# Two graph layers over one pass through a 64 MB adjacency matrix: turns of 256 rows for 512, runs of 2 KB for 1 KB

## The chip, the cores and the metric

The kernel runs on one core of one Trainium2 chip. Its engines work side by side and wait for each other through semaphores: TensorE (PE, with its weight loads listed apart as PEld), VectorE (DVE), ScalarE (ACT), GpSimd (POOL), and SyncE (SP), which here only issues transfers; POOL issues some too. All transfers run on the core's 16 DMA engines. The metric is the time of one execution on the device, in microseconds (us). Everything is computed in float32.

## The reference

`adj` is 4096 x 4096, mostly zero, with a full diagonal; `x` is 4096 x 128. Cut to what matters:

```
h   = relu(layernorm(x))
msg = h @ W0 + B
w   = where(adj < 1, exp(-(1/adj - 1)**2 / 0.5), 0)
x   = x + w @ msg                       # layer 0
h   = relu(layernorm(x))
A   = adj + I;  d = rowsum(A) ** -0.5
x   = x + relu((d[:,None] * A * d[None,:]) @ (h @ W1.T))    # layer 1
```

Layer 1's product needs `support = d * (h @ W1.T)` of all rows of x, and so layer 0 of all rows; both layers need every element of `adj`.

## The kernel before, in words

`adj` (64 MB) is read once. Its rows come in `G` = 8 turns of 512 rows. A turn has four pairs; `load(n)` on SP (L274) brings pair n, 512 rows by 1024 columns, as four DMAs of 512 KB, each into 32 of the 128 partitions of one of the `RAW` = 2 buffers `raw`, in contiguous runs of `W` = 256 floats (1 KB). A pair is two units u, each 512 x 512, a tile of 128 x 2048 floats. `UNITS` = 64.

For each unit DVE turns it in 32 x 32 blocks (`turn`, L648: `kept` <- `raw`, `KEPT` = 4 buffers), and masks it (`cut`, L663: `wt` <- `kept`, `WTS` = 6 buffers). ACT makes the weights in place in four passes (log L528, 1/adj L533, square L538, exp L547); for every second unit of the first three turns DVE does the square (`quad`, L669). PE multiplies the weights with `msg` into the PSUM bank `acc0` (`multiply_weights`, L377, `LAG` = 3 units behind). In turns 0 to 2 PE sums the rows of adj (L407); from turn 3 (`PE_SUMS`) DVE does, straight from `raw`, both units of a pair in one reduction (`row_sum`, L656).

When all 8 units of turn g-1 are in `acc0`, a chain of small steps makes 512 rows of `support` during turn g: ACT copies acc0 out (`copy_x1t`, L573), PE turns it (`turn_x1`, L430), DVE adds x and normalizes (`make_x1`, L745), PE turns and multiplies it (L436, L442), ACT copies and takes powers, DVE scales (`make_support`, L774).

Layer 1 uses the same adj tiles. A unit whose column block's support exists (`at_once`) is multiplied from `kept` (`mix_once`, L390). All others are stored to DRAM (`store`, L291, 1 MB each, 35 of them), read back later by POOL (L345) into one of `LATE` = 3 buffers `late`, or, at the end, into the parts of `raw`, and multiplied then (`mix_late`, L399) in places written out by hand (`JOBS`, `TAIL`). The PSUM banks at the end are turned back, scaled, passed through relu, added to x and written.

What sets the order is the order in which each engine's queue is written; no scheduler moves anything. `load(n)` waits until pair n-2 is turned, and from turn 3 on until its `row_sum` is done too. `turn(u)` waits until unit u-4 is out of `kept` (stored or multiplied). PE's next `acc0` sum waits for `copy_x1t`, and `turn_x1` waits in addition for `own_rows` (DVE, L736), which reads the row sums from the same bank.

## Time and profile before

| | |
|---|---|
| median of 3 runs | 662.49 us (662.48 to 664.77) |
| the profiled execution | 667.09 us, span 665.3 us |
| PE busy | 542.6 us, 82% |
| DVE busy | 485.1 us, 73% |
| ACT busy | 466.5 us, 70% |
| POOL busy | 39.6 us, 6% |
| mean granted TensorE clock | 0.921 of 2.4 GHz |
| DMA | 145.14 MB, mean 218 GB/s |

The span goes from the first to the last instruction of the profiled execution, and its own time is 1.8 us longer. It is 4.6 us above the median of the other runs. Busy time is the sum over the span, and says nothing about where an engine waits; a stage with its own limit has to be read by itself. Matmul ends are modelled, so starts are used below, not durations. An f32 matmul is two instructions in the trace and one in the program's order.

### The profile page before, as it was taken

The page shows a single profiled execution, that of the slowest core. Times are in us where ns is not written, and L with a number is a line of the kernel's source. Part 1 is how long each engine was busy: PE and PEld are TensorE (multiplying, and loading weights), DVE is VectorE, ACT ScalarE, POOL GpSimd, SP SyncE. Part 2 cuts the span into 40 slices and gives each one's busy share as a digit, 9 for nine tenths or more (in the row PEclk, how much of TensorE's full clock was granted, in tenths as well). Part 3 has the DMA queues.
Part 4 walks back from the last instruction along what each step waited for, and adds up shares of the span by engine and source line. Part 5 has one row for each costly group of instructions (what it writes and reads, how often), then busy time and mean ns, then how long its engine had stood idle before and what let it go on. Part 6 is the DMA issues. An engine that isn't in the chain of part 4 may idle for free.

```text
span 665.3 us, 4420 instructions
## 1 busy us (share of the span) xinstructions
PE 542.6 (82%) x1509; PEld 246.7 (37%) x1509; DVE 485.1 (73%) x555; ACT 466.5 (70%) x306; POOL 39.6 (6%) x68
## 2 busy tenths in 40 slices
PE   0548777699778975698496999699989999899995
PEld 0324423233233432243243434344435444344442
DVE  2899967796678997789596996699378956501156
ACT  0568968888859698969966996699596993750010
POOL 0432200000000000000000000000000000011100
PEclk9968797799778997989697999799999999999999
DMA  8999999999999599969998699969976971186713
GB/s 159 199 268 270 325 273 280 283 271 284 251 285 236 102 287 274 271 111 260 270 228 190 125 199 295 258 152 222 301 196 147 222 158 64 63 339 225 257 50 78
DMA packets 87193, 145.14 MB, mean 218 GB/s; under 512 B 4225, under 2 KB 78210, under 8 KB 78210
## 3 DMA queue, kind: packets, MB, share of 16 engines
q1 hardware_dynamic: 82130, 108.15, 71.3%
q0 software_dynamic: 5040, 36.70, 15.7%
q8 instruction: 12, 0.20, 0.1%
q14 instruction: 11, 0.09, 0.0%
HBM read 106.04 MB, written 38.80 MB: 218 GB/s over the span
## 4 chain that ended last, share of the span: by engine, by line
PE 30%; ACT 28%; DVE 17%; DMA 12%; issue 6%; SPq 6%; DVEq 0%
DMA raw<-in_adj_dram 12%; PE mix L399 10%; PE acc L377 9%; ACT wt L528 7%; ACT wt L547 7%; ACT wt L538 7%; ACT wt L533 7%; PE mix L390 6%; DVE kept L648 5%; SPq L281 5%; DVE wt L663 4%; DVE wt L669 2%; PE side L442 2%; PE acc L399 2%; PE side L399 1%
## 5 line engine op out<-in xcount | busy, mean ns | idle before, releaser
L377 PE MATMUL acc<-wt,msg 128*128 128x512 f32 x512 | 251.1, 637 | 35.2 <-ACT x1t L573 35.2
L528 ACT ACTIVATE wt<-wt 128x2048 f32<-128x2048 f32 x64 | 122.0, 1906 | 107.4 <-DVE wt L663 107.4
L648 DVE STREAM_TRANSPOSE kept<-raw 128x2048 f32<-128x2048 f32 x64 | 147.6, 2306 | 40.5 <-DMA raw<-in_adj_dram 27.5
L377 PEld LDWEIGHTS acc<-wt,msg 128*128 128x128 f32 x512 | 102.2, 206 | 172.7 <-issue 128.6
L663 DVE SCALAR_TENSOR_TENSOR wt<-kept 128x2048 f32<-128x2048 f32 x64 | 146.5, 2289 | 1.5
L533 ACT ACTIVATE wt<-wt 128x2048 f32<-128x2048 f32 x64 | 121.5, 1898 | 0.3
L390 PE MATMUL mix<-kept,support 128*128 128x512 f32 x224 | 101.5, 598 | 2.0 <-ACT mixed L589 1.7
L547 ACT ACTIVATE wt<-wt 128x2048 f32<-128x2048 f32 x52 | 98.5, 1895 | 0.0
L538 ACT ACTIVATE wt<-wt 128x2048 f32<-128x2048 f32 x52 | 98.5, 1894 | 0.0
L399 PE MATMUL mix<-late,support 128*128 128x512 f32 x200 | 90.8, 598 | 0.0
L656 DVE TENSOR_REDUCE rowpart<-raw 128x16 f32<-128x4096 f32 x20 | 87.6, 4378 | 0.0
L390 PEld LDWEIGHTS mix<-kept,support 128*128 128x128 f32 x224 | 42.2, 192 | 55.0 <-issue 53.0
L399 PEld LDWEIGHTS mix<-late,support 128*128 128x128 f32 x200 | 38.5, 193 | 48.0 <-issue 48.0
L745 DVE TENSOR_TENSOR x<-side,x 128x512 f32<-128x512 f32 x8 | 5.5, 691 | 65.1 <-PE side L430 65.1
L345 POOL DMA_DIRECT2D late<-adj_t_spill x27 | 14.4, 535 | 525.4 <-PE mix L399 425.4
L407 PE MATMUL mix<-kept,ones 128*32 128x512 f32 x192 | 30.8, 722 | 10.0 <-DVE kept L648 10.0
L442 PE MATMUL side<-w1t,hid_t 128*128 128x128 f32 x64 | 12.7, 361 | 25.8 <-ACT hid_t L585 25.8
L669 DVE SCALAR_TENSOR_TENSOR wt<-wt 128x2048 f32<-128x2048 f32 x12 | 27.4, 2282 | 0.0
L632 ACT COPY kept<-mix 128x512 f32<-128x512 f32 x6 | 3.5, 585 | 29.9 <-PE mix L399 26.6
L330 POOL TENSOR_SCALAR support<-x,mv 128x128 f32<-128x128 f32 x24 | 20.1, 856 | 48.2 <-DVE mv L688 48.2
L442 PEld LDWEIGHTS side<-w1t,hid_t 128*128 128x128 f32 x64 | 11.2, 259 | 31.7 <-ACT hid_t L585 30.8
L544 ACT ACTIVATE wt<-wt 128x2048 f32<-128x2048 f32 x12 | 22.7, 1895 | 0.0
(87 smaller groups left out, 247.0 us busy)
## 6 DMA issues: line engine op xcount, KB each, us to landing
raw<-in_adj_dram SPq DMA_DIRECT2D x128, 512.0 KB, 12.4
adj_t_spill<-kept SPq DMA_DIRECT2D x35, 1024.0 KB, 14.0
late<-adj_t_spill POOLq DMA_DIRECT2D x27, 1024.0 KB, 10.1
raw<-adj_t_spill POOLq DMA_DIRECT2D x8, 1024.0 KB, 6.1
x<-in_x_dram SPq DMA_DIRECT2D x32, 64.0 KB, 7.6
out_dram<-kept SPq DMA_DIRECT2D x32, 64.0 KB, 1.8
w_sb<-in_L_gnn_W_dram SPq DMA_DIRECT2D x1, 64.0 KB
late<-in_L_gnn_W_dram SPq DMA_DIRECT2D x1, 64.0 KB
```

The source lines that it names most:

```text
L377: mm = nc.tensor.matmul(acc0[:], msg[:, col(u) * T + k, :], wt[:, u % WTS, k, :], start=(first and k == 0), stop=(last and k == T - 1))
L390: mm = nc.tensor.matmul(once_bank[g][:], support[:, c * T + k, :], kept[:, u % KEPT, k, :], start=(first and k == 0), stop=False)
L399: mm = nc.tensor.matmul(bank[:], support[:, c * T + k, :], late_tile(slot)[:, k, :], start=(start and k == 0), stop=(stop and k == T - 1))
L442: mm = nc.tensor.matmul(side[:, a * P:(a + 1) * P], hid_t[:, a * P:(a + 1) * P], w1t[:], start=True, stop=True)
L528: nc.scalar.activation(v, v, ACT.Ln, bias=LN_GUARD).then_inc(ln_done, 1)
L533: nc.scalar.activation(v, v, ACT.Exp, scale=-1.0).then_inc(inv_done, 1)
L538: nc.scalar.activation(v, v, ACT.Square, bias=-1.0).then_inc(square_done, 1)
L547: nc.scalar.activation(v, v, ACT.Exp, scale=-2.0).then_inc(wt_done, 1)
L648: nc.vector.transpose(dst, src).then_inc(turned, 1)
L656: nc.vector.tensor_reduce(dst, src, AX_X, ALU.add).then_inc(summed, 1)
L663: nc.vector.scalar_tensor_tensor(out=wt[:, u % WTS], in0=v, scalar=CUTOFF, in1=v, op0=ALU.is_lt, op1=ALU.mult).then_inc(cut_done, 1)
L669: nc.vector.scalar_tensor_tensor(out=v, in0=v, scalar=-2.0, in1=v, op0=ALU.add, op1=ALU.mult).then_inc(quad_done, 1)
```

## The change

Rows now come in `G` = 16 turns of 256 rows. A turn has two loads l (`C2` = 2), each 256 rows by 2048 columns: still 2 MB in four DMAs into 32 partitions each, now in runs of 512 floats (2 KB). A load has two units, which are still 128 x 2048: `cut`, the passes on ACT and their buffers keep their size and number. `kept` has 2 buffers of a whole load; a load is turned in two halves (one for each k), each of which holds a part of all its eight 256 x 256 blocks. All 64 `turn` are shifted: the second half of load l stands at the head of unit 2l, the first half of load l+1 at the head of unit 2l+1. `row_sum` goes by halves, 40 of 2048 elements per partition in place of 20 of 4096, one behind each `cut` from turn 6 on.

A block of adj is multiplied at once only if its support is two turns old (c <= g-2). The others are stored in one DMA per load, up to 2 MB, and read back in pieces of one or two blocks (256 or 512 KB) into 6 smaller `late` buffers. `acc0` has two halves, one for each parity of the turn, so the next turn's sum no longer waits for this turn's copy. The chain's steps are respaced: copy, `own_rows`, `turn_x1` and `make_x1` in turn g+1, `multiply_support` and `make_support` in turn g+2. Every matmul of `acc0` and `mix` has 256 columns in place of 512, and there are twice as many. `LAG` is 2. At the start SP issues the weights' DMAs ahead of x and adj. The final relu moves from DVE to ACT.

```diff
-G = 8
-C4 = 4
+G = 16
+C2 = 2
-T = 4
-RAW, KEPT, WTS, LATE = 2, 4, 6, 3
-LAG = 3
+T = 2
+H = 8
+PART = 4
+RAW, KEPT, WTS, LATE = 2, 2, 6, 6
+LAG = 2
...
-PE_SUMS = 3
+PE_SUMS = 6
...
-            def load(n):
-                g = n // C4
-                if n >= RAW:
-                    if n - RAW >= PE_SUMS * C4:
-                        sp.wait_ge(summed, n - RAW + 1 - PE_SUMS * C4)
-                    sp.wait_ge(turned, 2 * (n - RAW + 1))
+            def load(l):
+                g = l // C2
+                if l >= RAW:
+                    sp.wait_ge(turned, 2 * (l - RAW) + 2)
+                    if l - RAW >= PE_SUMS * C2:
+                        sp.wait_ge(summed, 2 * (l - RAW + 1 - PE_SUMS * C2))
                 for q in range(Q):
-                    sp.dma_start(raw[q * B:(q + 1) * B, n % RAW],
-                                 adj_parts[g // 2, g % 2, col(2 * n) // 2, q]).then_inc(raw_loaded[n % RAW], 16)
+                    sp.dma_start(raw[q * B:(q + 1) * B, l % RAW],
+                                 adj_parts[g // H, g % H, c_of(l), q]).then_inc(raw_loaded[l % RAW], 16)
...
+                if u % 4 == 0 and g >= 2:
+                    pe.wait_ge(x1t_copied, g - 1)
+                for a in range(PART * T):
+                    mm = nc.tensor.matmul(acc0[:, g % 2, :], msg[:, blocks(u)[0] * T + a, :], wt[:, u % WTS, a, :],
+                                          start=(u % 4 == 0 and a == 0), stop=(u % 4 == 3 and a == PART * T - 1))
...
+                g, idx = u // 4, u % 4
+                l = u // 2
+                if u % 2 == 0:
+                    turn(l, 1)
+                elif l + 1 < LOADS:
+                    turn(l + 1, 0)
+                cut(u)
+                if u >= 1 and squared_by_dve(u - 1):
                     quad(u - 1)
-                if idx % 2 == 1 and g >= PE_SUMS:
-                    row_sum(u // 2)
+                if g >= PE_SUMS:
+                    row_sum(l, u % 2)
...
+                if g >= 2 and idx == 1:
+                    make_support(g - 2)
                 if g >= 1 and idx == 3:
                     own_rows(g - 1)
-                if g >= 1 and idx == 5:
                     make_x1(g - 1)
-                if g >= 1 and idx == 7:
-                    make_support(g - 1)
-                if g >= PE_SUMS:
-                    cut(u)
```

Two places carry most of it. First DVE in the second half of the program, from one `row_sum` to the first turn of the same `raw` buffer's next contents. Before (L648 turn, L663 cut, L656 row_sum of a whole pair, L736 and L739 own_rows; `raw_loaded` is the wait for adj):

```order
L656 TENSOR_REDUCE rowpart<-raw 128x4x4 [waits quads_summed]
L663 SCALAR_TENSOR_TENSOR wt<-kept 128x2048 [waits acc0_done,turned]
L648 STREAM_TRANSPOSE kept<-raw 128x16x4x32 [waits once_done,raw_loaded1]
L663 SCALAR_TENSOR_TENSOR wt<-kept 128x2048 [waits acc0_done,turned]
L648 STREAM_TRANSPOSE kept<-raw 128x16x4x32 [waits once_done]
L656 TENSOR_REDUCE rowpart<-raw 128x4x4
L736 TENSOR_TENSOR rowown<-side,own_quad 128x64 [waits newton,quads_summed]
L739 TENSOR_REDUCE pows<-rowown 128x4 [waits rows_owned]
L663 SCALAR_TENSOR_TENSOR wt<-kept 128x2048 [waits acc0_done,turned]
L648 STREAM_TRANSPOSE kept<-raw 128x16x4x32 [waits once_done,raw_loaded0]
```

Of the change (L728 turn, L747 cut, L736 row_sum of half a load, L757 to L857 make_support):

```order
L728 STREAM_TRANSPOSE kept<-raw 128x8x8x32 [waits once_done,spilled1,raw_loaded1]
L747 SCALAR_TENSOR_TENSOR wt<-kept 128x2048 [waits acc0_done,turned]
L736 TENSOR_REDUCE rowpart<-raw 128x2x2
L757 TENSOR_TENSOR tmp<-inv 128x4 [waits pows_exp]
L759 SCALAR_TENSOR_TENSOR tmp<-tmp,pows 128x4 [waits newton]
L762 SCALAR_TENSOR_TENSOR inv<-tmp,inv 128x4 [waits newton]
...
L728 STREAM_TRANSPOSE kept<-raw 128x8x8x32
L747 SCALAR_TENSOR_TENSOR wt<-kept 128x2048 [waits acc0_done,turned]
L736 TENSOR_REDUCE rowpart<-raw 128x2x2
L728 STREAM_TRANSPOSE kept<-raw 128x8x8x32 [waits spilled0,raw_loaded0]
```

Before, buffer 0 is done at the first row, and turned again at the last: three cuts, two turns and another whole reduction stand between them. In the change the last read of buffer 0 is the third row, one turn ahead of which stands the first turn of buffer 1; from there to buffer 0's next turn stand one turn, one cut, half a reduction and a chain step.

Second SP at the same stage: what each load waits for. Before:

```order
L291 DMA adj_t_spill<-kept 128x2048 [waits turned] x2
L281 DMA raw<-in_adj_dram 32x16x256 [waits turned,summed]
L281 DMA raw<-in_adj_dram 32x16x256 x3
L291 DMA adj_t_spill<-kept 128x2048 [waits turned]
L281 DMA raw<-in_adj_dram 32x16x256 [waits turned,summed]
L281 DMA raw<-in_adj_dram 32x16x256 x3
```

Of the change:

```order
L323 DMA adj_t_spill<-kept 128x1024 [waits turned]
L309 DMA raw<-in_adj_dram 32x8x512 [waits summed,turned]
L309 DMA raw<-in_adj_dram 32x8x512 x3
L323 DMA adj_t_spill<-kept 128x4096 [waits turned]
L309 DMA raw<-in_adj_dram 32x8x512 [waits summed,turned]
L309 DMA raw<-in_adj_dram 32x8x512 x3
```

The waits have the same names and each load has four DMAs of 32 partitions in both; what moved is the place on DVE at which `summed` is reached.

Third PE at the last support but one (L413 weights, L426 mix at once, L438 mix late, L478 turn_x1, L484 turn_hid). Before, the corresponding chain (L430) stands in the middle of the last turn:

```order
L430 MATMUL side<-ident,x1t 128x128 [waits rows_owned,x1t_copied]
L430 MATMUL side<-ident,x1t 128x128 x3
L377 MATMUL acc<-wt,msg 128x512 [waits wt_done]
L377 MATMUL acc<-wt,msg 128x512 x3
L390 MATMUL mix<-kept,support 128x512 [waits turned]
L390 MATMUL mix<-kept,support 128x512 x3
```

Of the change:

```order
L478 MATMUL side<-ident,x1t 128x128 [waits rows_owned,x1t_copied]
L478 MATMUL side<-ident,x1t 128x128
L438 MATMUL mix<-late,support 128x256 [waits sup_done,late_loaded4]
L438 MATMUL mix<-late,support 128x256 x3
L438 MATMUL mix<-late,support 128x256 [waits sup_done,late_loaded5]
L438 MATMUL mix<-late,support 128x256 x3
L426 MATMUL mix<-kept,support 128x256 [waits sup_done,turned]
L426 MATMUL mix<-kept,support 128x256 x3
L413 MATMUL acc<-wt,msg 128x256 [waits wt_done]
L413 MATMUL acc<-wt,msg 128x256 x7
L484 MATMUL side<-ident,hid 128x128 [waits hid_done]
```

The first row waits for `own_rows`, which DVE in the change reaches only after the last unit's cut and row sum; the weights of the last three units and the whole tail are behind it on PE.

## Rows read from the trace of the kernel before

**Rows 1.** The chain of waits by engine and line, whole span (page, part 4).

```profile
PE 30%; ACT 28%; DVE 17%; DMA 12%; issue 6%; SPq 6%; DVEq 0%
```

**Rows 2.** Busy time by stage: us, busy of PE, PEld, DVE, ACT, POOL, PEclk, DMA share, GB/s.

```profile
88.00:220.00 132.00, 107.20 (x334) 41.60 (x333) 101.95 (x91) 105.86 (x67) 1.05 (x2) 0.87 1.06 270
220.00:573.00 353.00, 304.99 (x745) 139.29 (x743) 286.62 (x220) 286.74 (x177) 9.51 (x18) 0.94 0.86 205
336.80:407.20 70.40, 63.11 (x155) 28.91 (x154) 58.14 (x48) 58.97 (x36) 1.58 (x3) 0.95 0.88 196
```

**Rows 3.** Waits: who waited for whom, us in total, times, longest.

```profile
ACT wt L528 <- DVE wt L663: 107.4, 31, 11.4
DVE x L745 <- PE side L430: 65.1, 7, 24.0
PE acc L377 <- ACT x1t L573: 35.2, 5, 11.4
```

**Rows 4.** DVE's timeline from a row sum to the same buffer's next turn.

```profile
366.49 4.38 DVE L656 TENSOR_REDUCE rowpart<-raw 128x16 f32<-128x4096 f32 x1
370.78 2.28 DVE L663 SCALAR_TENSOR_TENSOR wt<-kept 128x2048 f32<-128x2048 f32 x1
372.98 2.30 DVE L648 STREAM_TRANSPOSE kept<-raw 128x2048 f32<-128x2048 f32 x1
375.32 2.29 DVE L663 SCALAR_TENSOR_TENSOR wt<-kept 128x2048 f32<-128x2048 f32 x1
...
386.63 2.31 DVE L648 STREAM_TRANSPOSE kept<-raw 128x2048 f32<-128x2048 f32 x1
```

**Rows 5.** L281's issues and landings for one load, window 370 to 372.6.

```profile
L281 SPq DMA_DIRECT2D raw<-in_adj_dram x4: 312/488/490, 370.9 to 372.3; - x4
DMA to landing us min/median/max: 5.0/8.4/12.5
```

**Rows 6.** The same for two other loads, windows 299 to 302 and 512 to 520.

```profile
L281 SPq DMA_DIRECT2D raw<-in_adj_dram x4: 312/488/499, 299.1 to 300.5; - x4
DMA to landing us min/median/max: 5.0/8.4/11.5
...
L281 SPq DMA_DIRECT2D raw<-in_adj_dram x4: 311/486/489, 515.3 to 516.7; - x4
DMA to landing us min/median/max: 5.0/8.4/14.2
```

**Rows 7.** Transfers of 373 to 381 us: adj alone, runs of 1 KB.

```profile
DMA packets 1627, 1.62 MB, mean 202 GB/s; under 512 B 48, under 2 KB 1627, under 8 KB 1627
```

**Rows 8.** Transfers of 31 to 35 us: x alone, runs of 512 B, also 32 partitions.

```profile
DMA packets 1812, 0.84 MB, mean 209 GB/s; under 512 B 201, under 2 KB 1811, under 8 KB 1811
```

**Rows 9.** Transfers of 586 to 594 us: reads of the spill, 8 KB, 128 partitions.

```profile
DMA packets 467, 3.43 MB, mean 429 GB/s; under 512 B 48, under 2 KB 48, under 8 KB 48
```

**Rows 10.** DVE's timeline, where turn 2 ends and row sums begin.

```profile
218.13 2.31 DVE L648 STREAM_TRANSPOSE kept<-raw 128x2048 f32<-128x2048 f32 x1 [1.44 <-DMA raw<-in_adj_dram]
220.36 2.25 DVE L669 SCALAR_TENSOR_TENSOR wt<-wt 128x2048 f32<-128x2048 f32 x1
222.53 2.28 DVE L663 SCALAR_TENSOR_TENSOR wt<-kept 128x2048 f32<-128x2048 f32 x1
...
226.96 4.38 DVE L656 TENSOR_REDUCE rowpart<-raw 128x16 f32<-128x4096 f32 x1
```

**Rows 11.** DVE's timeline, the last cut.

```profile
577.50 2.28 DVE L663 SCALAR_TENSOR_TENSOR wt<-kept 128x2048 f32<-128x2048 f32 x1
```

**Rows 12.** The chain's end, in order of time.

```profile
649.20 3.44 PE acc L399 x8
652.63 0.44 PE mix L488 x4
653.07 3.45 PE side L399 x8
656.52 0.02 issue
661.01 0.69 DVE kept L824
```

**Rows 13.** PE's timeline in the tail: 128-column matmuls and what follows.

```profile
618.48 1.05 PE L442 MATMUL side<-w1t,hid_t 128*128 128x128 f32 x8
619.37 1.45 PE L399 MATMUL acc<-raw,support 128*128 128x512 f32 x3
```

**Rows 14.** ACT's timeline: two passes in a row.

```profile
363.45 1.90 ACT L533 ACTIVATE wt<-wt 128x2048 f32<-128x2048 f32 x1
365.25 1.89 ACT L547 ACTIVATE wt<-wt 128x2048 f32<-128x2048 f32 x1
```

More of the change, by code:

```diff
@@ L99, in late_slot @@
         return j % LATE
-    tail = [(len(IN_TURN) + i) % LATE for i in range(LATE)] + [LATE + i for i in range(2 * RAW)]
+    tail = [(len(IN_TURN) + i) % LATE for i in range(LATE)] + [LATE + i for i in range(4 * RAW)]
     return tail[(j - len(IN_TURN)) % len(tail)]
@@ L367, in multiply_msg @@
                 last.then_inc(m_multiplied, 1)
             def multiply_weights(u):
-                first, last = u % G == 0, u % G == G - 1
+                g = u // 4
                 pe.wait_ge(wt_done, u + 1)
-                if u < G and u % 2 == 0:
-                    pe.wait_ge(msg_done, u // 2 + 1)
-                if first and u >= G:
-                    pe.wait_ge(x1t_copied, u // G)
-                for k in range(T):
-                    mm = nc.tensor.matmul(acc0[:], msg[:, col(u) * T + k, :], wt[:, u % WTS, k, :],
-                                          start=(first and k == 0), stop=(last and k == T - 1))
+                if g == 0:
+                    pe.wait_ge(msg_done, blocks(u)[0] // PART + 1)
@@ L384, in mix_once @@
[L384 to L391 removed]
+                r = u // 4
@@ new lines, in mix_once @@
+                pe.wait_ge(turned, 2 * (u // 2) + 2)
+                pe.wait_ge(sup_done, at_once(u)[-1] + 1)
+                first = r % 2 == 0 and once_count(u // 2 - 1) + (u % 2 and bool(at_once(u - 1))) == once_count(2 * r - 1)
+                if first and r >= 12:
+                    pe.wait_ge(evicted, r // 2 - 5)
+                for c in at_once(u):
+                    for k in range(T):
+                        mm = nc.tensor.matmul(turn_bank[r // 2][:, r % 2, :], support[:, c * T + k, :],
+                                              kept[:, u // 2 % KEPT, c % H, k, :],
+                                              start=(first and c == at_once(u)[0] and k == 0), stop=False)
@@ L401, in mix_late @@
                 mm.then_inc(late_done, 1)
             def sum_tiles(u):
-                pe.wait_ge(turned, u + 1)
-                bank = sum_bank[u // G]
-                for k in range(T):
-                    mm = nc.tensor.matmul(bank[k * B:(k + 1) * B, :], ones[:], kept[:, u % KEPT, k, :],
-                                          start=(u % G == 0), stop=(u % G == G - 1))
+                pe.wait_ge(turned, 2 * (u // 2) + 2)
+                g = u // 4
+                if u % 4 == 0 and g >= 2:
+                    pe.wait_ge(sums_copied, g - 1)
@@ L462, in _ @@
                 if g < PE_SUMS:
                     sum_tiles(u)
-                if at_once(u) and idx < G - 1 and not (g >= 6 and idx == 0):
+                if at_once(u):
                     mix_once(u)
-                if g >= 1 and idx == 4:
-                    turn_x1(g - 1)
+                if g >= 1 and idx == 2:
+                    if g <= PE_SUMS:
+                        add_sums(g - 1)
+                    else:
+                        add_quads(g - 1)
                 if u >= LAG:
@@ new lines, in copy_h0 @@
+            def copy_h0(s):
+                act.wait_ge(h0_turned, s + 1)
+                if s >= 1:
+                    act.wait_ge(m_multiplied, s)
+                nc.scalar.copy(h0_t[0], h0_bank[0][:].rearrange("p r j -> p (r j)"))
+                nc.scalar.copy(h0_t[1], h0_bank[1][:].rearrange("p r j -> p (r j)")).then_inc(h0_t_done, 1)
+            def copy_sums(g):
+                act.wait_ge(tiles_summed, 4 * (g + 1))
+                if g >= 1:
+                    act.wait_ge(rows_added, g)
+                for k in range(T):
+                    last = nc.scalar.copy(in_tiles(sums[:, k]), by_tile(sum_bank[g % 2][:, k, :]))
+                last.then_inc(sums_copied, 1)
@@ new lines, in relu_out @@
+            def relu_out(i):
+                b = ENDS[i]
+                act.wait_ge(out_summed, i + 1)
+                for a in range(2 * T):
+                    v = fin[i % 4][:, a * D:(a + 1) * D]
+                    n = b * 2 * T + a
+                    last = nc.scalar.activation(v, v, ACT.Relu, scale=dinv[:, n:n + 1])
+                last.then_inc(out_relu, 1)
+            for i, b in enumerate(ENDS):
+                if b >= 2:
+                    take_mix(i)
+                if i >= 2:
+                    relu_out(i - 2)
```

646 lines of the change are left out of this document (341 added, 305 removed), and 4 rows, old and new, of the table JOBS.

## The prediction, made before the result was known

> **What bounds the kernel now.** I read the chain of waits first: no engine holds a third of it [rows 1], so the stages have to be read apart. From 88 to 220 us the DMA share is 1.06 (over 1, since transfers of two queues overlap) while DVE and ACT are busy 102 and 106 of 132 us [rows 2]: transfers bind. From 220 to 573 us it is 0.86, and PE, DVE and ACT have 305, 287 and 287 of 353 us; one turn lasts 70.4 us with PE 63.1, ACT 59.0 and DVE 58.1 in it. What is missing there is in the table of waits [rows 3]: DVE stands in `make_x1` for PE's `turn_x1` (65.1 us in 7 waits), so the next cut is late and ACT idles (107.4 us, up to 11.4 a time); PE waits 35.2 us for acc0's copy. After 573 us PE works off a backlog.
>
> The wait that does not show is the one for adj. On DVE's timeline [rows 4] a row sum starts at 366.49, the next instruction at 370.78, and the turn that needs the same buffer again at 386.63: 15.8 us. The load issued at 370.9 landed at 372.3 + 12.5 = 384.8, 13.9 us after its first issue [rows 5]; two others took 300.5 + 11.5 - 299.1 = 12.9 us and 516.7 + 14.2 - 515.3 = 15.6 us [rows 6]. The mean is 14.1 us. So the load is hidden, with under 2 us to spare.
>
> **The change: the load's cover.** From turn 6 on, load l+2 is issued when DVE has finished the second half sum of load l. In DVE's new order that half sum stands behind the first turn of load l+1, which waits for load l+1 to land. So load l+2 cannot be issued before load l+1 has landed: the two buffers no longer overlap, and one load is in flight at a time. The period of a load is its latency, plus a turn, a cut and a half sum. By starts in [rows 4] a turn takes 2.34 us, a cut 2.21, a whole sum 4.29, so a half 2.15: together 6.7 us. What else DVE has in a period (another 6.7 us, and a chain step of 1.4 or about 3 us) lies inside the latency.
>
> **The latency with 2 KB runs.** The trace has no 2 KB runs. Adj's 1 KB runs alone moved at 202 GB/s [rows 7]; x's runs of 512 B at 209 GB/s [rows 8]. Halving the run cost nothing, so I see no cost per run that doubling it could save. Both go into 32 partitions per DMA, as the change's loads still do. The spill's reads, 8 KB runs into 128 partitions, made 429 GB/s [rows 9]; they differ in two things, and the pair above speaks for the partitions. A load of 2.10 MB at 202 GB/s is 10.4 us, at 209 it is 10.0: I take 0.4 us off, 14.1 - 0.4 = 13.7 us, and a period of 20.4 us. Bounds: below, 8 KB's rate, 2.10 / 0.429 = 4.9 us in place of 10.4, latency 8.6 us, period 15.3 (DVE's own work is then 2 x 6.7 + 2.3 = 15.7, and binds); above, no gain from runs, 20.8. By the spread of [rows 5, 6], which comes from other transfers in flight, the period is 12.5 + 6.7 = 19.2 to 15.6 + 6.7 = 22.3.
>
> The Trainium skill ("SBUF — State Buffer", section "Door 1: The DMA port swizzle") says that a DMA into partitions 0 to 31 reaches 8 of the 16 ports, 189 GB/s measured at 1 MiB and about 218 at best, whatever its runs. The trace agrees with 202 and 209. By its 218 GB/s a load's transfer would be an estimated 9.6 us and the period 19.9, 9 us less in the sum.
>
> **How often it is paid.** Loads 14 to 31 wait for half sums. From the issue of load 14 to that of load 31 are 17 periods, 347 us; load 31 lands 13.7 us later; then DVE has turn, cut, half sum (6.7), `make_support` (1.4), the same three (6.7) and the last cut (2.2): 17.0 us.
>
> **When it begins.** Before, unit 24 is turned at 218.1 us, waiting for adj, and the first row sum starts at 226.96 [rows 10]. Up to there the change moves as many bytes: the same 24 units of adj, and 86 spilled blocks of 0.25 MB (21.5 MB) for 21 stores of 1 MB. The weights' three DMAs now ahead of adj cost 1.4 us, and turn 0 has the same work on x in half as many units, some 2 us that the transfers don't cover. With 8 x 0.4 us back from the runs I put that landing at 218. Then stand turn and cut (4.5), a chain step (3), turn, cut, quad and half sum (6.7 + 2.2), and a turn, cut and half sum (6.7), and slack of 1 for the load between: 240 us. The last cut ends at 240 + 347 + 13.7 + 17.0 = 618 us; before it ends at 577.5 + 2.3 = 579.8 [rows 11].
>
> **The tail.** In the change `turn_x1` of turn 14 waits for `own_rows`, which follows the last cut by a half sum and 0.6 us: PE stands until 2.8 us after the cut. Behind it are 10 blocks and three units' weights, and then TAIL with 57 blocks. Eight 512-column instructions take 3.44 us [rows 12], 430 ns each. A unit's weights are 3.44 us as before; a block is 4 of 256 columns, 0.86. 67 x 0.86 + 3 x 3.44 = 68 us, with 5 for the small matmuls and the output's 32 transposes, 2.8 before, and 3 for half clock after the stand: 79. From the last product's end to the end it is now 665.3 - 656.5 = 8.8 us [rows 12]; with eight output DMAs for four, 9. So 88 us, against 665.3 - 579.8 = 85.5.
>
> Sum: 618 + 88 = 706 us of span; before 665.3.
>
> **What I cost at nothing.** Matmuls of 256 columns: in the tail eight of 128 columns start at 618.48, and what follows at 619.37 [rows 13], 111 ns each where 430 / 4 is 107. So a weight load per 128 columns is hidden, and 4 ns is the price of an instruction. 1024 more of them are 4 us of PE, which waits anyway; 0.5 in the tail are counted. ACT: passes start 1.80 us apart [rows 14], 14.4 us a load with 1 for small copies: under 20.4. DVE's extra small steps, 2 us a turn: inside the latency. If the cover went, ACT and DVE would bind at about 15.7 us a load. The doubled acc0 and the chain's wider spacing do remove the waits of [rows 3], up to 11.4 us in each of five turns, but nobody gets that time: DVE now stands for adj instead. PE has 13.8 us of weights in a turn, up to 26 blocks (22.4) and 1: 37 us in the last turns, against two periods of 40.8.
>
> **Rivals.** First, *2 KB runs are much faster*, which ends below before. If the 1 KB run's 81 ns (1024 B at a sixteenth of 202 GB/s) and the 8 KB run's 305 ns (429) lie on one line, 2 KB is 113 ns, 290 GB/s, 7.2 us: period 17.2, in the early stage 15 us less (ACT then holds it), so 225 + 292 + 10.5 + 17 + 88 = 633. At 429 GB/s: 218 + 267 + 9 + 17 + 88 = 599, plus some 10 for PE's last turns. It decides from a period below 18.6 us, a load's transfer under 8.6 us or 244 GB/s. For it speaks that runs and partitions change together in [rows 7, 9]; against it [rows 7, 8]. Chance 0.19.
>
> Second, *PE becomes the bound* in the last turns: after each stand for `own_rows` it runs at half clock for a while (PEclk is 0.94 on the mean of the middle stage [rows 2] with shorter stands). Five more us in 37 pass 40.8: up to 20 us in four turns, 715 to 735. Chance 0.10.
>
> Third, *adj's rows are read at a wider step*: one DMA now steps 4 MB from run to run, before 1 MB. Adj with 1 MB steps and x with 512 B steps move alike [rows 7, 8], so I see no cost. If it halved the rate, a period would be 20.4 + 10 = 30, and the sum 240 + 35 + 510 + 24 + 17 + 88 = 914. Chance 0.03. The Trainium skill ("DMA: Bandwidth & Descriptors", section "Latency and other measured facts") lists 164 GB/s at a row pitch of 2 MiB and 103 at 4 MiB for copies within DRAM; no run here shows it yet.
>
> Fourth, *a middle case*: the transfer falls to 8.5 to 9 us and nothing is left to tell: 655 to 670. Chance 0.05.
>
> **The numbers.** The profiled execution's own time is 667.1, 1.8 above its span, and 4.6 above the median of 662.5. So 706 + 1.8 - 4.6 = 703. The forecast as worked out has chance 0.63; its own range takes the period's 19.2 to 22.3: 18 x -1.2 = -22 and 18 x 1.9 = +34, 681 to 737. For 8 in 10 the range goes down to the first rival's upper case, 640, and up to 737. Faster than before by over 0.5% (about what a measurement of this kernel can tell from no change) 0.21, within it 0.04, slower 0.75.
>
> **What would show it.** Right: from about 240 us L309's groups of four are issued 20 us apart, each right behind a second half sum, never two in flight; the last of each lands some 12 us after its issue; DVE's wait for raw, 27.5 us before, is then 18 times about 4.7, some 85 us; the waits of [rows 3] at `acc` and `x` are gone or small, ACT's wait for the cut is larger; the last cut ends near 618. Wrong: adj alone moving at 250 GB/s or more, issues 16 to 18 us apart, or PE busy through the second half. The step I trust least is the rate of 2 KB runs; each microsecond there is 18 in the sum.

## The result, and the profile after

| | before | after |
|---|---|---|
| median | 663.57 us (4 runs, 662.48 to 664.77) | 766.53 us (4 runs, 763.73 to 772.95) |
| profiled execution, span | 667.09, 665.3 us | 766.08, 764.3 us |
| PE, DVE, ACT busy | 542.6, 485.1, 466.5 us | 567.4, 489.3, 484.1 us |
| mean granted TensorE clock | 0.921 | 0.876 |

The ratio is 1.157, 95% interval 1.149 to 1.164: slower, as forecast, but 64 us beyond the forecast's 703 and outside its range of 640 to 737. Medians in the experiments leave out executions in a slower state, such as one of `e16` with 939.3 us at a granted clock of 0.56, the only one of that kernel with a trace. Rows of after, beside [rows 1] and [rows 3]. The page's chain of waits, by engine and by line:

```profile
DMA 50%; DVE 21%; PE 9%; issue 8%; SPq 8%; POOL 2%; ACT 1%; DVEq 0%; ACTq 0%
DMA raw<-in_adj_dram 49%; DVE wt L747 8%; DVE rowpart L736 6%; SPq L309 5%; PE mix L438 4%; DVE kept L728 3%; SPq L346 2%; POOL support L364 2%; PE acc L413 1%; PE acc L438 1%; PE mix L400 1%; DVE msg L795 1%; PE mix L391 0%; PE side L478 0%; SPq L317 0%
```

The waits (us in total, times, longest):

```profile
DVE kept L728 <- DMA raw<-in_adj_dram: 165.7, 28, 9.6
ACT wt L581 <- DVE wt L747: 157.3, 43, 13.2
PE side L478 <- DVE rowown L819: 72.8, 9, 13.2
```

Before, no engine held a third of the chain; now transfers hold half and one line's load nearly all of it. What the change was built to remove is gone: PE's wait for acc0 has no row, and DVE's for PE in `make_x1` is 14.6 us where it was 65.1. DVE stands for adj instead, ACT for DVE, and PE for `own_rows`.

One period in order of time, the chain of waits from 401 to 423 us (start, us, what):

```profile
401.26 2.25 DVE wt L747
403.51 2.21 DVE rowpart L736
...
405.78 0.31 SPq L309
...
407.12 15.73 DMA raw<-in_adj_dram
...
422.91 2.20 issue
```

A cut, the second half sum, and only then the next load's four issues; DVE's next turn starts at 422.88, 17.1 us after the first issue. SP's timeline gives the periods. The first of these groups is load 14, the last load 31:

```profile
248.58 2.74 SPq L309 DMA_DIRECT2D raw<-in_adj_dram  x4
...
635.37 2.66 SPq L309 DMA_DIRECT2D raw<-in_adj_dram  x4
```

(635.37 - 248.58) / 17 = 22.75 us a load, where 20.4 was forecast. DVE's timeline from load 31's landing to the last cut:

```profile
652.66 2.31 DVE L728 STREAM_TRANSPOSE kept<-raw 128x2048 f32<-128x2048 f32 x1 [8.16 <-DMA raw<-in_adj_dram]
...
667.38 2.28 DVE L747 SCALAR_TENSOR_TENSOR wt<-kept 128x2048 f32<-128x2048 f32 x1
```

and the end, PE's timeline (the last product), SP's (the output) and DVE's (the last steps):

```profile
738.03 7.07 PE L438 MATMUL side<-raw,support 128*128 128x256 f32 x32
```
```profile
731.70 30.96 SPq L346 DMA_DIRECT2D out_dram<-kept  x64
```
```profile
748.88 0.69 DVE L909 TENSOR_TENSOR kept<-side,support 128x512 f32<-128x512 f32 x1 [1.78 <-DMA out_dram<-kept]
...
750.91 0.69 DVE L916 TENSOR_TENSOR kept<-kept,x 128x512 f32<-128x512 f32 x1 [0.74 <-ACT kept L702]
```

DVE is done at 751.6, but SP still issues 32 KB writes until 762.7, 484 ns apart. The span against my sum, term by term:

| term | forecast | measured | off by |
|---|---|---|---|
| issue of load 14 | 240 | 248.6 | +8.6 |
| 17 periods | 347 | 386.8 | +39.8 |
| load 31, issue to turn | 13.7 | 17.3 | +3.6 |
| from there to the last cut's end | 17.0 | 17.0 | 0 |
| last cut to the last product | 79 | 75.3 | -3.7 |
| last product to the end | 9 | 19.4 | +10.4 |
| span | 706 | 764.3 | +58.3 |

So the mechanism stands (one load in flight, a period of latency plus 6.7 us) and two sizes are wrong: the latency, and the end. The experiments ask whether the mechanism is really the cost, what lengthens the latency, and what holds the end. The kernel before was run beside each group; medians of it were 662.2 to 664.0 us, and ratios are to it.

### The profile page after: what moved, and what is told of

Same layout as the page of the kernel before. It is cut to its first block, busy times and chain, and to the rows that moved or that the text cites. A ratio compares the mean times of both kernels' runs of the same rounds, so it can differ in the third digit from the quotient of the medians.

```text
span 764.3 us, 6963 instructions
## 1 busy us (share of the span) xinstructions
PE 567.4 (74%) x2567; PEld 462.4 (60%) x2567; DVE 489.3 (64%) x604; ACT 484.1 (63%) x387; POOL 67.7 (9%) x124
## 3 DMA queue, kind: packets, MB, share of 16 engines
q0 software_dynamic: 10992, 39.07, 16.8%
## 4 chain that ended last, share of the span: by engine, by line
DMA 50%; DVE 21%; PE 9%; issue 8%; SPq 8%; POOL 2%; ACT 1%; DVEq 0%; ACTq 0%
DMA raw<-in_adj_dram 49%; DVE wt L747 8%; DVE rowpart L736 6%; SPq L309 5%; PE mix L438 4%; DVE kept L728 3%; SPq L346 2%; POOL support L364 2%; PE acc L413 1%; PE acc L438 1%; PE mix L400 1%; DVE msg L795 1%; PE mix L391 0%; PE side L478 0%; SPq L317 0%
## 5 line engine op out<-in xcount | busy, mean ns | idle before, releaser
L728 DVE STREAM_TRANSPOSE kept<-raw 128x2048 f32<-128x2048 f32 x64 | 147.5, 2306 | 165.7 <-DMA raw<-in_adj_dram 165.7
L413 PE MATMUL acc<-wt,msg 128*128 128x256 f32 x1024 | 243.8, 393 | 8.6 <-ACT wt L600 6.5
L413 PEld LDWEIGHTS acc<-wt,msg 128*128 128x128 f32 x1024 | 199.1, 197 | 49.3 <-issue 9.4
L747 DVE SCALAR_TENSOR_TENSOR wt<-kept 128x2048 f32<-128x2048 f32 x64 | 145.4, 2272 | 1.1
L438 PE MATMUL mix<-late,support 128*128 128x256 f32 x464 | 124.2, 422 | 0.0
L426 PE MATMUL mix<-kept,support 128*128 128x256 f32 x420 | 105.1, 405 | 20.3 <-DVE kept L728 14.6
L426 PEld LDWEIGHTS mix<-kept,support 128*128 128x128 f32 x420 | 85.6, 206 | 39.3 <-DVE kept L728 15.8
L438 PEld LDWEIGHTS mix<-late,support 128*128 128x128 f32 x464 | 97.4, 217 | 14.3
L736 DVE TENSOR_REDUCE rowpart<-raw 128x4 f32<-128x2048 f32 x40 | 91.1, 2278 | 0.0
L380 POOL DMA_DIRECT2D late<-adj_t_spill x68 | 36.2, 533 | 609.0 <-PE mix L438 512.0
L478 PE MATMUL side<-ident,x1t 128*128 128x128 f32 x32 | 9.3, 387 | 101.6 <-DVE rowown L819 72.8
L478 PEld LDWEIGHTS side<-ident,x1t 128*128 128x128 f32 x32 | 4.3, 184 | 107.3 <-issue 107.2
L391 PE MATMUL mix<-ident,support 128*128 128x128 f32 x32 | 6.7, 381 | 22.6 <-POOL support L364 15.6
L597 ACT ACTIVATE wt<-wt 128x2048 f32<-128x2048 f32 x12 | 22.8, 1902 | 0.0
```

Of the source, the lines that this page charges most:

```text
L380: pool.dma_start(late_tile(slot)[:, 0:n].rearrange("p c k j -> p (c k j)"), spill[r, c // H][:, h * BLK:(h + n) * BLK]).then_inc(late_load ...
L413: mm = nc.tensor.matmul(acc0[:, g % 2, :], msg[:, blocks(u)[0] * T + a, :], wt[:, u % WTS, a, :], start=(u % 4 == 0 and a == 0), stop=(u % ...
L426: mm = nc.tensor.matmul(turn_bank[r // 2][:, r % 2, :], support[:, c * T + k, :], kept[:, u // 2 % KEPT, c % H, k, :], start=(first and c ...
L438: mm = nc.tensor.matmul(bank[:, r % 2, :], support[:, (c + b) * T + k, :], late_tile(slot)[:, b, k, :], start=(start and b == 0 and k == 0 ...
L728: nc.vector.transpose(dst, src).then_inc(turned, 1)
L736: nc.vector.tensor_reduce(dst, src, AX_X, ALU.add).then_inc(summed, 1)
```

## Experiments

**Is it the cover? One row moved on DVE.** `e1_sum_first`:

```diff
+                if g >= PE_SUMS and u % 2 == 1:
+                    row_sum(l, 1)
                 if u % 2 == 0:
                     turn(l, 1)
                 elif l + 1 < LOADS:
                     turn(l + 1, 0)
                 cut(u)
...
-                if g >= PE_SUMS:
-                    row_sum(l, u % 2)
+                if g >= PE_SUMS and u % 2 == 0:
+                    row_sum(l, 0)
```

> The changed kernel with one row moved on DVE: the second half sum of load l stands ahead of the first turn of load l+1, so load l+2 can be issued while load l+1 is still in flight. Theory A (the lost cover costs the time; the engines would allow less): the period of a load falls from 22.75 us to 16 to 17 us, set by DVE's own 15.7 us and ACT's 15; over 17 periods that is 100 us less, 655 to 680 us. Rival B (a load's transfer is slow by itself, so two in flight only share the engines): the period stays above 20 us and the time at 720 to 766 us.

Measured: 692.6 us, ratio 1.044 (1.036 to 1.051). Its waits:

```profile
DVE kept L728 <- DMA raw<-in_adj_dram: 61.5, 19, 8.9
ACT wt L581 <- DVE wt L747: 66.4, 26, 12.5
```

and loads 14 and 31 on SP:

```profile
240.24 2.79 SPq L309 DMA_DIRECT2D raw<-in_adj_dram  x4
...
552.52 2.72 SPq L309 DMA_DIRECT2D raw<-in_adj_dram  x4
```

The period is 312.3 / 17 = 18.4 us and 74 of the 103 lost us are back. The place of that one row is most of the loss. But the period isn't the 16 to 17 us of theory A: it lies between A and rival B. What holds it there this run doesn't say. A slow load is a small part of it: with nearer rows on top (`e8` below) the period is (538.41 - 236.45) / 17 = 17.8 us, and only with another order on PE (`e15`) is it (519.88 - 230.81) / 17 = 17.0.

**The same loss made in the kernel before.** `e2_before_held`:

```diff
-                    sp.wait_ge(turned, 2 * (n - RAW + 1))
+                    sp.wait_ge(turned, 2 * n if n - RAW >= PE_SUMS * C4 else 2 * (n - RAW + 1))
```

> The kernel before, with nothing but a later issue of its loads: from turn 3 on, load n waits until both units of pair n-1 are turned, so that one load is in flight at a time and 6.8 us of DVE's work (turn, cut, turn) stand between a landing and the next issue, about as in the change. Runs stay 1 KB and the rest of the kernel is untouched. If the cover alone costs the time: period 14.1 + 6.8 = 20.9 us, 240 + 17 x 20.9 + 14 + 13.5 + 85.5 = 708 us of span, about 705 us. If a load that is alone takes 16 us in this form too (so 2 KB runs aren't to blame): period 22.8, about 740 us. If the cover doesn't matter: 663 us.

Measured: 713.3 us, ratio 1.076 (1.068 to 1.084). SP's timeline from load 14's row on; 14 loads lie ahead of the last row shown, whose group is itself four loads:

```profile
232.09 2.51 SPq L281 DMA_DIRECT2D raw<-in_adj_dram  x4
...
525.08 66.13 SPq L281 DMA_DIRECT2D raw<-in_adj_dram  x16
```

(525.08 - 232.09) / 14 = 20.9 us: the period expected of this run, with the 14.1 us of latency that [rows 5, 6] give; the time is 8 us above the 705 expected. So the rule "latency plus DVE's work" and its 14.1 us hold where the runs are 1 KB and their rows 1 MB apart. In the change the latency is about 16.

**Is it the run's length?** `e3_1k_runs`, the change with each load in two halves of its columns:

```diff
-                for q in range(Q):
-                    sp.dma_start(raw[q * B:(q + 1) * B, l % RAW],
-                                 adj_parts[g // H, g % H, c_of(l), q]).then_inc(raw_loaded[l % RAW], 16)
+                for s in range(2):
+                    v = slice(s * W // 2, (s + 1) * W // 2)
+                    for q in range(Q):
+                        sp.dma_start(raw[q * B:(q + 1) * B, l % RAW, :, v],
+                                     adj_parts[g // H, g % H, c_of(l), q][:, :, v]).then_inc(raw_loaded[l % RAW], 16)
...
-                    dve.wait_ge(raw_loaded[l % RAW], 64 * (l // RAW + 1))
+                    dve.wait_ge(raw_loaded[l % RAW], 128 * (l // RAW + 1))
```

> The changed kernel with each of its loads cut into eight DMAs of 1 KB runs for four of 2 KB, with the same bytes, places and waits. Theory A (the latency of 16 us comes from what else is in flight and from the tail of the slowest engine, not from the run's length): the period stays at 22 to 24 us and the time at 755 to 790 us, more rather than less since SP issues four more DMAs of 0.4 us. Rival C (2 KB runs, or what goes with them, are slower than 1 KB): the period falls by some 2.3 us and the time to about 725 us.

Measured: 778.4 us, ratio 1.172 (1.162 to 1.183). No gain: not the length. **The loads by themselves**, `e4_loads_alone`, one 2 MB load at a time (L50 2 KB runs 8 MB apart, L55 1 KB and 1 MB, L61 1 KB and 8 MB, L66 2 KB and 2 MB, L71 and L78 the first two with a store). L50, L61 and L71 were meant to be the change's form, and the expectation calls them 4 MB. They aren't: their pattern is

```python
adj_w = adj.rearrange("(e g i) (C q w) -> g C q i e w", e=8, g=16, i=B, C=2, q=4)
```

in which one step of `e` is 16 x 32 = 512 rows of 16 KB, 8 MB. In the change it is 8 x 32 = 256 rows, 4 MB. So no run measures a 4 MB step by itself, and where the expectations from here on say 4 MB of a load alone, 8 MB was run.

> Measures the disputed cost by itself; it computes nothing and writes zeros. Loads of 2 MB into 32 partitions per DMA, one at a time, nothing else in flight: 2 KB runs 4 MB apart (the change's), 1 KB runs 1 MB apart (the one before), 1 KB runs 4 MB apart (eight DMAs), 2 KB runs 2 MB apart; then the first two forms again with a 2 MB store from 128 partitions issued right behind each load. If run length is to blame for the late landing: 14 us and more for 2 KB against 12 for 1 KB. If the step is: 4 MB slower than 1 MB at either length. If only what else is in flight is: all four near 12 us alone, and 15 to 18 us with the store.

SP's timeline; six loads a row, four for L66:

```profile
18.94 73.37 SPq L50 DMA_DIRECT2D wide<-in_adj_dram  x24
103.33 61.62 SPq L55 DMA_DIRECT2D narrow<-in_adj_dram  x24
175.06 72.46 SPq L61 DMA_DIRECT2D wide<-in_adj_dram  x48
255.88 37.61 SPq L66 DMA_DIRECT2D wide<-in_adj_dram  x16
303.31 2.63 SPq L71 DMA_DIRECT2D wide<-in_adj_dram  x4
...
418.41 1.90 SPq L78 DMA_DIRECT2D narrow<-in_adj_dram  x4
...
518.95 0.41 SPq L83 DMA_DIRECT2D out_dram<-zeros  x1
```

From one row's start to the next's, divided by its loads: 14.07 us for 2 KB and 8 MB, 11.96 for 1 KB and 1 MB, 13.47 for 1 KB and 8 MB, 11.86 for 2 KB and 2 MB. 2 KB runs are no faster than 1 KB; 8 MB between a partition's eight rows costs 1.5 to 2.2 us a load. With a 2 MB store beside it the 8 MB form takes (418.41 - 303.31) / 6 = 19.2 us and the one before (518.95 - 418.41) / 6 = 16.8: traffic adds 5 to both, and the difference stays. That the change's 4 MB cost as much is the guess that the next run tests in the kernel.

**The step in the kernel.** `e5_near_rows`, order as in the change:

```diff
-        adj_parts = adj.rearrange("(R e h i) (C q w) -> R h C q i e w", e=8, h=H, i=B, C=C2, q=Q)
+        adj_parts = adj.rearrange("(R h e i) (C q w) -> R h C q i e w", e=8, h=H, i=B, C=C2, q=Q)
```

> The changed kernel, reading other rows: the 256 rows of a turn stand next to each other in adj, so that one DMA steps 512 KB from run to run and not 4 MB; all else, the order on DVE too, is the change's. It computes with the rows of adj in another order, so its output is another one. By itself a load with a 4 MB step took 14.1 us from issue to issue and one with 2 MB 11.9 (the run of loads alone). Theory A (the step is the mis-sized part of the latency): the period falls from 22.75 by some 2.2 us, over 17 periods and load 31 about 40 us, and 5 more in the stage that transfers bind: 715 to 730 us. Rival B (the late landing comes from stores and spill reads in flight or from uneven engines): 755 to 770 us.

Measured: 725.5 us, ratio 1.094 (1.087 to 1.100). Loads 14 and 31:

```profile
239.51 1.80 SPq L309 DMA_DIRECT2D raw<-in_adj_dram  x4
...
593.11 1.79 SPq L309 DMA_DIRECT2D raw<-in_adj_dram  x4
```

Load 14 is issued at 239.5, 9.1 us earlier than in the change (I had said 240), and the period is 353.6 / 17 = 20.80 us (I had said 20.4). The step alone is 9.1 + 17 x 1.95 = 42 of the 58 us that I missed; the medians differ by 41.0 us. Of the 9.1 us some may be chance: DVE first turns load 12 at 225.7 us in the change and at 216.7 here, but at 221.8 in `e1`, whose program is the change's up to there.

**Other forms of a load**, `e6_forms_alone` and `e7_first_by_row`. The second is `e1` with:

```diff
-        adj_parts = adj.rearrange("(R e h i) (C q w) -> R h C q i e w", e=8, h=H, i=B, C=C2, q=Q)
+        adj_parts = adj.rearrange("(R e h i) (C q w) -> R h C e q i w", e=8, h=H, i=B, C=C2, q=Q)
...
-                for q in range(Q):
-                    sp.dma_start(raw[q * B:(q + 1) * B, l % RAW],
-                                 adj_parts[g // H, g % H, c_of(l), q]).then_inc(raw_loaded[l % RAW], 16)
+                for e in range(8):
+                    sp.dma_start(raw[:, l % RAW, e],
+                                 adj_parts[g // H, g % H, c_of(l), e]).then_inc(raw_loaded[l % RAW], 16)
```

and with DVE's wait counting to 128 for 64, as in `e3`.

> Loads of 2 MB in 2 KB runs by themselves again, six of each form, computing nothing: the change's (rows 4 MB apart, four DMAs of 32 partitions); 256 neighbouring rows (512 KB apart, same four DMAs); rows in pairs of 512 KB within 8 MB, eight DMAs of 32 partitions; the change's rows with one DMA per run of all 128 partitions (eight DMAs, neighbouring descriptors 2 or 16 KB apart); and two of the change's and two of the near loads in flight at once. If the step costs: the first takes 14.1 us, the second 11.9 or less. If the 32 partitions of a DMA hold the rate at about 200 GB/s: the form by all 128 partitions takes 7 to 9 us in place of 14; if the step or the whole of the engines holds it, 11 us or more. Two near loads at once, if the 200 GB/s are one load's own limit: under 20 us for both; if a shared one: 21 us and more.

> The change with the second half sum ahead of the next load's turn, as in the run that gave 692.6 us, and with each load as eight DMAs, one per row of all 128 partitions, for four of 32 partitions and eight rows. The same output as the change. If the form removes the cost of the 4 MB step or of the 32 partitions: DVE's wait for adj, 61.5 us there, falls to 20 or less: 655 to 675 us. If eight issues on SP (some 3.5 us a load) or the same rate as before eat it: 690 to 705 us.

`e6` on SP: six repeats in each of L53 (`adj_w` as in `e4`, 8 MB apart and not the change's 4), L58 (512 KB apart), L65 (pairs), L70 (one DMA per row of L53's), L76 and L83 (two of the first, two of the second at once):

```profile
18.95 73.44 SPq L53 DMA_DIRECT2D wide<-in_adj_dram  x24
103.07 62.90 SPq L58 DMA_DIRECT2D wide<-in_adj_dram  x24
175.95 63.67 SPq L65 DMA_DIRECT2D wide<-in_adj_dram  x48
247.66 130.52 SPq L70 DMA_DIRECT2D wide<-in_adj_dram  x48
388.94 128.00 SPq L76 DMA_DIRECT2D wide<-in_adj_dram  x48
533.49 112.61 SPq L83 DMA_DIRECT2D wide<-in_adj_dram  x48
664.06 0.42 SPq L87 DMA_DIRECT2D out_dram<-zeros  x1
```

14.0, 12.1, 11.9, 23.5, and 24.1 and 21.8 for two at once (12.0 and 10.9 each). The form in pairs is as fast as near rows, although each of its eight DMAs steps 8 MB from run to run too; it has four runs per partition for eight, and the near row of each pair is in another DMA. So a wide step by itself doesn't make a load slow. Whether the number of rows at that step or the near rows in between make the difference, no run separates. Two loads at once gain little: in this form, four DMAs of 32 partitions a load, both together move at most 193 GB/s, so the overlap hides a load's latency and makes no rate. One DMA per row is by far the slowest: `e7` took 966.3 us, ratio 1.456. `e6` from 300 to 340 us, transfers:

```profile
DMA packets 1890, 3.76 MB, mean 94 GB/s; under 512 B 56, under 2 KB 56, under 8 KB 1890
```

with the 16 engines busy 0.25 of the time. The Trainium skill ("DMA: Bandwidth & Descriptors", section "Why a DMA increments its semaphore by 16 and not by 1") says that the engines a DMA uses are the largest number up to 16 that divides the slowest dimension of both its patterns. In this form adj's slowest dimension is the quarter, 4, so four of 16; the trace agrees with the share of 0.25. I had expected 7 to 9 us there from the number of partitions, and hadn't looked at the pattern's outer dimension.

**Both causes away.** `e8_first_and_near` is `e1` with the line of `e5`.

> Both causes taken away at once: the second half sum ahead of the next load's turn, and neighbouring rows (512 KB steps; adj's rows in another order, so another output). If the step and the lost cover are all that the change lost on adj, DVE's wait for it falls from 61.5 to some 20 us, and the time to 655 to 675 us, about that of the kernel before. Rival (what is left is PE or the tail): 680 to 692 us, with PE in the chain from 560 us on in either case.

Measured: 677.1 us, ratio 1.019 (1.012 to 1.025), just above the expected range, with an output in another order as in `e5`. DVE waits 35.3 us for adj in 15 waits, and the top wait of a working engine is another:

```profile
ACT x1t L626 <- PE acc L413: 59.5, 9, 14.0
```

ACT's copy of acc0 stands ahead of its passes and waits for PE's last weights of the turn, which stand behind the blocks mixed at once.

**The same with the reference's output.** `e9_paired_rows`: strips of 32 rows in neighbouring pairs (h, k, i for k, h, i in adj, x and out). A load is then eight DMAs, one for each k and q, and two runs of x and of the output merge into one DMA each. The patterns, and the load:

```diff
-        adj_parts = adj.rearrange("(R e h i) (C q w) -> R h C q i e w", e=8, h=H, i=B, C=C2, q=Q)
+        adj_parts = adj.rearrange("(R e h k i) (C q w) -> R h C q k i e w", e=Q, h=H, k=T, i=B, C=C2, q=Q)
...
-        out_parts = out.rearrange("(C q k h i) d -> C q k i h d", C=C2, q=Q, k=T, h=H, i=B)
+        out_parts = out.rearrange("(C q h k i) d -> C q i (h k) d", C=C2, q=Q, k=T, h=H, i=B)
...
+                for k in range(T):
+                    for q in range(Q):
+                        dst = raw[q * B:(q + 1) * B, l % RAW].rearrange("p (e k) w -> p k e w", k=T)[:, k]
+                        sp.dma_start(dst, adj_parts[g // H, g % H, c_of(l), q, k]).then_inc(raw_loaded[l % RAW], 16)
```

> The second half sum ahead of the next load's turn, and another order of rows and columns within a turn: 32-row strips in neighbouring pairs (rows h, k, i instead of k, h, i), in adj, x and out alike, so the output is the reference's. A load is then eight DMAs with four runs per partition, the form that took 11.95 us alone against 14.02; x needs four DMAs a part for eight, and a bank of the output four DMAs for eight (32 in all for 64). Theory: adj as fast as with neighbouring rows (677.4 us), and the end after PE's last product, 19 us with 64 output DMAs at 0.47 us each on SP, shorter by 8 to 10: 665 to 670 us. Rival (eight issues per load, some 3.5 us on SP, eat what the step gives): 675 to 690 us.

Measured: 663.1 us, ratio 1.001 (0.998 to 1.005), no different from before, and just below the expected range. The period, (533.87 - 229.50) / 17 = 17.9 us, is that of near rows. Last product to the end is 661.9 - 652.2 = 9.7 us, the 9 that I had given it, with 32 output DMAs.

**The end.** `e10_two_queues` (on `e9`) and `e12_out_by_two` (on the change) let POOL issue half of the output's DMAs; `e14_out_by_act` (on the change) lets ACT issue one half and leaves SP the other. ACT's part of `e14`:

```diff
+            def write_half(i):
+                b = ENDS[i]
+                act.wait_ge(out_done, i + 1)
+                tiles = fin[i % 4].rearrange("p (h k d) -> p k h d", h=2, k=T)
+                for q in range(Q):
+                    h = 2 * b % H
+                    act.dma_start(out_parts[2 * b // H, q, 1][:, h:h + 2],
+                                  tiles[q * B:(q + 1) * B, 1]).then_inc(out_written[i % 4], 16)
```

> The same, and half of the 32 output DMAs issued by POOL, whose queue is empty by then. If SP's issues still hold the end: 2 to 4 us less than the run before. If the last bank's own chain (turn, sum, relu, sum, write) holds it: no change.

> The changed kernel itself, with nothing but half of its 64 output DMAs issued by POOL. From PE's last product to the end it takes 19.4 us where I had forecast 9, with SP issuing from 731.7 us for 31 us. If the issues on SP are that difference: 8 to 10 us less, 756 to 759 us. If the writes themselves are slow: no change, 766 us.

> The changed kernel, half of whose 64 output DMAs are issued by ACT, each behind its bank's last step. With POOL as the second issuer the last write was issued 8 us earlier than in the change, but landed 12 us after its issue. If SP's issues are what my 9 us for the end left out and POOL's own transfers the reason that it didn't show: 756 to 759 us. If the writes are slow whoever issues them: 766 us.

Measured: 669.5 (ratio 1.013, 1.008 to 1.019), 768.0 (1.162, 1.154 to 1.169) and 755.1 us (1.143, 1.137 to 1.149). ACT's share gives 11 us: the end is SP's issues, as the 64 DMAs at 484 ns say. POOL's gives nothing in the change and costs 6 us in `e10`. In `e12` the last issue ends 8.6 us behind the last product (756.2 against 747.7), where it was 17.8 in the change: what the shorter queue gives is lost behind it. POOL's writes land 2 us after their issue, not 12 as the expectation of `e14` has it, which counted to the end of the program. The last issues and their landing are over at 758 us, but the program ends at 768.1:

```profile
753.60 2.63 POOL L387 DMA_DIRECT2D out_dram<-kept  x5
```
```profile
DMA to landing us min/median/max: 1.8/1.9/2.8
```

What runs in the last 10 us has no row; in `e10` the last POOL issue is at 655 and the end at 666.9. Why the program ends so late is open.

**What is left: PE's order.** `e11_weights_first` (on `e10`), `e13_paired_weights` (on `e9`) and `e15_weights_all` (on `e9`):

```diff
+                if u >= LAG:
+                    multiply_weights(u - LAG)
                 if at_once(u):
                     mix_once(u)
...
-                if u >= LAG:
-                    multiply_weights(u - LAG)
```

That is `e15`; in the other two it is done at the second unit of a turn only. `e16_all_three` is `e13` with half of the output issued by ACT.

> The same as the run before, and at the second unit of each turn PE does the last weights of the turn before ahead of the blocks mixed at once. In the run with near rows ACT stood 49.6 us for PE in 6 copies of acc0 between 240 and 600 us. If that stand is on the path: up to 3.45 us less in each of some 9 turns, at most 15 us and more likely 5 in all. If PE is the bound there, its order doesn't matter: no change; a loss of 2 to 5 us if the kept buffer, free 3.45 us later, holds DVE.

> Half sum first, rows in neighbouring pairs, all output DMAs on SP (663.1 us), and PE's last weights of a turn ahead of the blocks mixed at once. With POOL's half of the output this order gave 6.5 us (669.5 to 663.0). If that gain is ACT's shorter stand for acc0, it adds up: 656 to 658 us. If it was chance or POOL's end: 663 us.

> The same with the weights ahead of the blocks mixed at once in every unit, not in one of four. If ACT waits for PE's weights only at the copy of acc0: no more gain than with one of four, 656 to 660 us. If the kept buffer, free 3.45 us later each time, holds DVE's next turn: 665 to 680 us.

> Half sum first, paired rows, weights first in one unit of four, and the 32 output DMAs half on SP and half on ACT. After DVE's last step the end still takes 4.9 us with all of them on SP; four issues of 0.47 us become two: 1 to 2 us less than the run without it, 654 to 657 us, or no change if ACT's issues delay its own copies.

Measured: 663.0 us (ratio 0.999, 0.995 to 1.003), which is 6.5 below `e10`; 652.1 (0.986, 0.981 to 0.990); **641.4** (0.969, 0.965 to 0.973); 650.3 (0.984, 0.979 to 0.989). `e13` gave more than I had said, and `e15`, of which I expected nothing or a loss, 11 us more. The waits of its profiled execution (648.1 us):

```profile
ACT wt L579 <- DVE wt L745: 65.9, 29, 10.0
DVE kept L726 <- DMA raw<-in_adj_dram: 41.3, 16, 6.3
PE acc L411 <- ACT wt L598: 25.8, 9, 3.5
```

ACT's wait for PE at the copy, 59.5 us in 8 waits in `e9`, is 37.3 in 7 in `e13` and 21.5 in 5 here:

```profile
ACT x1t L624 <- PE acc L411: 21.5, 5, 10.4
```

PE waits more for ACT's weights instead, 3.5 us at most a time. `e16` and `e13` can't be told apart: the 1 to 2 us expected are within the intervals. With the order of DVE and PE and the rows changed, the change's design beats the kernel before by 3%. Whether the kernel before would gain from PE's other order too, no run shows.

## Why the prediction was right, and where it was wrong

- **Direction and mechanism: right, and shown.** That the second half sum behind the next load's turn leaves one load in flight was the forecast's core. `e1` takes only that away and gives back 74 us; `e2` puts only that into the kernel before and costs 49.
- **The failing step is the latency term**, "14.1 - 0.4 = 13.7 us, and a period of 20.4 us". It measured about 16.0 (22.75 - 6.7), 2.3 more, 18 times paid. The 0.4 us of gain from longer runs isn't there: 11.86 against 11.96 alone, and 20.80 us for the period with near rows, which is 14.1 + 6.7. The rest, 1.95 us a period, is the step that I had as the third rival, with the right place and chance 0.03, but priced only at "half the rate". "Adj with 1 MB steps and x with 512 B steps move alike, so I see no cost" read a trend from two points that both lie below the step in question; and x's own runs are 32 KB apart in a partition, 512 B is the distance of neighbouring partitions. Between "no cost" and "halved" lay the truth, a latency of 16.0 us with the 4 MB step and 14.1 without it, and the range didn't hold it. The Trainium skill ("DMA: Bandwidth & Descriptors", section "Latency and other measured facts") has 207 GB/s at a 512 KiB pitch and 103 at 4 and 8 MiB for copies within DRAM of 128 partitions. Here, in loads of 32 partitions whose neighbouring partitions are 16 KB apart and whose own rows are 4 MB apart, the measurement decides: the latency is 14% longer (16.0 against 14.1 us), not twice as long; alone, at 8 MB, a load takes 14.0 us against 12.1, and in eight DMAs of four runs 11.9. Why eight runs at a wide step are slower is open. Had I given the ground between no cost and halved a price and a chance, the range would have held the time.
- **Issue of load 14 (240):** DVE's work from load 12's first turn to this issue was right, 22 us forecast and 22.8 measured (248.6 - 225.7). Load 12 was late: 218 forecast, 225.7 measured, 216.7 with near rows.
- **Load 31's landing to the last cut, 17.0 us:** right.
- **Tail: 88 for 94.6.** PE's part, 79 forecast, 75.3: PE stood 0.75 us for `own_rows` where I had 2.8, and its granted clock was 1.00 from 669 to 745 us, so the 3 us for half clock were not paid. The end, 9 forecast, 19.4. "With eight output DMAs for four, 9" took a number of DMAs per bank from the code and no price for their issue. 64 at 484 ns are 31 us on one queue, behind banks that end within 20 us (731.7 to 751.6). Shown by `e14` and `e9`.
- **Costed at nothing:** right but for the 4 MB step above. Between 248 and 652 us no piece of the chain of after is PE's or ACT's, so neither the 256-column products nor ACT's passes set the period. Once the loads are repaired, PE's order matters, which before the change's waits had hidden.
- **DVE's wait for adj:** "18 times about 4.7, some 85 us". By the table of waits cut at 255 us it is 129.4 us in 18 waits from there on, 7.2 each: the count is right, and 2.5 more each is the latency. 36.4 us in 10 waits lie ahead of 255 us, and the 85 left them out.
- **Rival 1 (2 KB much faster):** refuted alone and in the kernel. **Rival 2 (PE bound in the last turns):** PE had work left after the last cut as planned, and no part of the loss. **Rival 4:** no.
- **Two slips beside the sum.** The period of 19.9 us and the 9 us less, from an estimated transfer of 9.6 us, come out as 20.0 and 7 (10.4 - 9.6 = 0.8 off the 14.1). And a DMA share over 1 needs no two queues: while one queue alone loads in `e4` (106 to 113 us) it is 1.11.

## What to carry to other kernels

With two buffers, a load's cover is decided by the last reader of a buffer, and whether that reader stands ahead of or behind the wait for the other buffer: list both on the engine's queue before anything else. When a tiling changes, work out three numbers of each transfer anew, not the run's length alone: the distance between a partition's rows and how many rows one DMA reads at that distance, the outer dimension of the pattern, and the count of DMAs times the time of an issue. And print the steps of a test's own pattern: the loads run alone here had twice the step of the kernel that they stood for, and only the run in the kernel, `e5`, priced its 4 MB. A repair can expose the next order: after the loads, PE's two lines swapped were worth 22 us together.

## What the runs showed of the hardware

- Loads of 2 MB in four DMAs of 32 partitions, eight 2 KB runs a partition, in the kernel: a period of 22.75 us with the runs 4 MB apart, 20.80 with 512 KB (`e5`).
- The same alone: 14.0 us with the runs 8 MB apart, 11.9 to 12.1 at 512 KB, 1 MB (in 1 KB runs) and 2 MB; as eight DMAs of four runs, also 8 MB apart but with the near row of each in another DMA, 11.9.
- A DMA of all 128 partitions whose DRAM pattern has an outer dimension of 4 keeps the 16 engines busy 0.25 of the time, 94 GB/s (`e6`).
- Two such loads at once, each of four DMAs into 32 partitions, take 24.1 or 21.8 us, one alone 14.0 or 12.1: 193 GB/s together at best.
- In the two runs traced in which POOL issues output up to the end (`e10`, `e12`), the program ends 9 to 10 us after the last write has landed; where SP or ACT issues the last one, it ends less than 2 us after that issue.
